# Expert visits of two half tiles of 64 rows, in two column tiles of TensorE with the weights moving

## The chip, the cores and the metric

One core of a Trainium2 chip runs the whole program in one launch. The metric is the device time in microseconds (us) of one execution; everything is in 32-bit floats.

## The reference, cut to what matters

A small vision model: patches are embedded (1184 tokens of 256 numbers: 32 images of 37), one layer of attention is added, then a mixture of experts:

```python
scores = sigmoid(x @ gate_weight.T)             # 32 experts in 4 groups; 6 of them chosen per token: topidx
g = einsum('th,ehi->tei', x, w_gate)            # hidden size 128
u = einsum('th,ehi->tei', x, w_up)
eo = einsum('tei,eih->teh', silu(g) * u, w_down)
routed = einsum('te,teh->th', cw, eo)           # cw: weight of the 6 chosen experts, else 0
shared = silu(x @ shared_w_gate) * (x @ shared_w_up) @ shared_w_down
lg = topidx[:, 0] // 2                          # one of 16 anchor experts, hidden size 64
anchor = ...                                    # the same form, with the weights of expert lg
out = routed + shared + 0.1 * anchor
```

So 7 x 1184 = 8288 (token, expert) pairs are computed: 7104 routed ones and 1184 anchor ones. How many pairs an expert gets is known only on the chip.

## The kernel before, in words

**Up to the experts** (about the first 200 us). Attention runs over 6 blocks of two tiles of 111 tokens. VectorE ranks the chosen experts block by block (`choose`, `place`), and GpSimd scatters each normed token row, with its weights and its destination rows, into `rows_d` in DRAM, where each of 48 lists (32 experts, 16 anchors) has a place for 1184 rows: 77 indirect DMAs (line 457). Before that SyncE has filled the first 256 rows of every list with zeros (line 378), and it loads all expert weights into `W` in SBUF: part early (line 380), the rest once the attention's buffers are dead (lines 392 and 398).

**The table** (lines 1441 to 1526, VectorE). From the counts of the 48 lists it works out, for each of 112 tiles of 128 rows, which weights it takes, where its rows start in `rows_d`, and which of its rows are valid. TensorE turns the columns into rows (`table_rows`, line 711), VectorE copies them to the SBUF table (line 1530, `table_ok`), and all engines read it into registers with `entry` (line 319, a TENSOR_LOAD on the queue of the engine). TensorE meanwhile finishes the shared expert and keeps itself busy (`stay_busy`) up to the first tile.

**The tiles.** 25 anchor tiles come first, then 87 routed ones: 24 full ones of one expert (F), and 32 packed ones (M) whose rows belong to several experts and which are summed from visits (M and 31 extra X). All the 128 rows of one tile meet the weights of one expert; in a visit of a packed tile the rows of the others are masked out by a weight of 0. For each tile i:

- SyncE loads 128 rows into one of 6 buffers `G` (`load_rows`, line 413), once TensorE has turned, and VectorE has read, the tile six before it; the first routed tile also waits for all scatters.
- TensorE turns the rows (`turn_rows`, 2 transposes, line 812), then computes gates and ups (`up`, line 823: the weights are stationary, the 128 turned rows move; 4 matmuls of 128 columns, 2 for an anchor), and one step later the down product (`down`, line 838: hidden values stationary, 256 columns of weights move).
- ScalarE copies the up weights of tile i+2 from `W` to `UPW` (`copy_up`, line 981), the turned rows from PSUM to `GT` (line 985), computes silu (line 990), and, for F tiles, weighs the result (line 995).
- VectorE multiplies silu and up (`hidden`, line 1597), takes the weights and destinations out of `G` (`take_columns`, lines 1566 and 1574), and adds the weighed result to the sums (`accumulate`, line 1589).
- GpSimd sends the sums, when complete, to `sums_d` in DRAM with an indirect DMA (line 483, 66 sends).

The order on TensorE is written out: `up(i)`, `turn_rows(i + 2)`, `down(i - 1)`. A 32-bit matmul stands in the trace as two records (a transpose as one).

**The end.** SyncE reads the seven results of each token back (`load_part`, line 419), one of them already 16 tiles before the end, VectorE adds them (line 1626), and the output is stored.

Of the kernel before, what the change touches and what calls it, by code (L numbers as in the profile page):

```python
# [17 lines left out]
F32 = mybir.dt.float32  # L18
I32 = mybir.dt.int32
# [42 lines left out]
DUMMY_ROW = P + LISTS * LIST_ROWS  # L62
# [7 lines left out]
ROWS_PACKED = -(-TOKENS * TOPK // P)  # L70
LAST_FILLED = TOKENS * TOPK % P
FULL = -(-(TOKENS * TOPK - EXPERTS * (P - 1)) // P)
MIXED = ROWS_PACKED - FULL
EXTRAS = EXPERTS - 1
ANCHOR_PACKED = -(-TOKENS // P)
ANCHOR_TILES = ANCHOR_PACKED + ANCHORS - 1
KINDS = "A" * ANCHOR_TILES + "FFX" * 12 + "XM" * 6 + "XMM" * 13
XT = len(KINDS)
INDEX = [KINDS[:i].count(k) for i, k in enumerate(KINDS)]
TILE_AXIS, EXTRA_AXIS = 1000, 2000  # L80
RING = D + 1
GB = 6
PL = 3 * EXPERTS + ANCHORS


def routed(i):
    return KINDS[i] != "A"


def summed(i):  # L90

    return KINDS[i] != "F"


def sums_before(i):
    return sum(summed(k) for k in range(i))


def copied_by_act(i):
    return KINDS[i] != "F"  # L100


def copies_before(i):
    return sum(copied_by_act(k) == copied_by_act(i) for k in range(i))


def number_of(i):

    return {"A": 0, "F": TILE_AXIS, "M": TILE_AXIS + FULL, "X": EXTRA_AXIS}[KINDS[i]] + INDEX[i]


FIRST_ROUTED = ANCHOR_TILES
EARLY_COLS = 19482
TRI4 = 3 * LISTS
SMALL = TRI4 + 23
PIECES = [[(0, 4), (4, 8), (8, NT)]] * (CHOICES - 1) + [[(0, 4), (4, 7), (7, 9), (9, 10), (10, NT)]]
assert KINDS.count("F") == FULL and KINDS.count("M") == MIXED and KINDS.count("X") == EXTRAS
assert all(KINDS[:i].count("X") >= min(EXTRAS, INDEX[i] + 1) for i in range(XT) if KINDS[i] == "M")
assert FULL * D <= ANCHOR_COLS and XT <= P
# [4 lines left out]
def build(nc, pt, wt, posr, brow, wqkv, wo, wg1, wg2, lnwb, gwt, gbias, sgu, sd, wx,  # L124
          ident_c, cmask_c, turn_c, parity_c, cs_c, before_c, small_c, out):
    with ExitStack() as ctx:
# [56 lines left out]
        def dense(*shape):  # L183
# [5 lines left out]
            if len(shape) == 2:  # L189
# [16 lines left out]
        mixed = spent[:, 0:MIXED * RING]  # L206
        mixed_rows = mixed.bitcast(I32)
# [5 lines left out]
        of_lists = small[:, 0:3 * LISTS].rearrange("p (q l) -> p q l", q=3)  # L213
        iota_a, base0, tri4 = small[:, LISTS:LISTS + ANCHORS], small[:, 2 * LISTS:3 * LISTS], small[:, TRI4:TRI4 + 16]
        pcol, number, of_number, tile_number, spare_row, last_tile, first_w = (small[:, TRI4 + 16 + q:TRI4 + 17 + q]
                                                                                  for q in range(7))
        ring = sb("ring", [P, ANCHOR_PACKED * RING])
        h = sb("h", [P, NT, D])
        ring_rows = ring[:, :].bitcast(I32)
        token_row = sb("token_row", [P, 2, NT], I32)  # L220
        to_rows = sb("to_rows", [P, NT])
        spare = sb("spare", [P, 2])
# [32 lines left out]
        whole = sb("whole", [P, 2 * LISTS], I32)  # L255
        tcol = sb("tcol", [P, 24])
        valid = turn
# [3 lines left out]
        def later(n):  # L261
# [6 lines left out]
        GT = later(2 * D).rearrange("p (u k s) -> p u k s", u=2, k=KC)  # L268
        S = later(2 * P).rearrange("p (u s) -> p u s", u=2)
        H = later(2 * P).rearrange("p (u s) -> p u s", u=2)  # L270
        tabs = e_sb[:, 0:at[0]]
        edges = later(2 * P).rearrange("p (u s) -> p u s", u=2)
        H_anchor = edges
        UPW = sb("UPW", [P, 2, UP_COLS])
        wcol = sb("wcol", [P, XT])
        tok_full = sb("tok_full", [P, FULL], I32)
        Y = W[:, 0:FULL * D].rearrange("p (f d) -> p f d", d=D)
        parts = W[0:TP, 0:CHOICES * NT * D].rearrange("p (c t d) -> p c t d", c=CHOICES, t=NT)

        B = [ctx.enter_context(nc.psum_tensor(f"B{i}", [P, 512], F32)) for i in range(8)]  # L280

        rows_d = nc.dram_tensor("rows_d", [DUMMY_ROW + 2 * P, ROW], F32).ap()
        sums_d = nc.dram_tensor("sums_d", [SPARE_ROW + P, D], F32).ap()
# [22 lines left out]
        g_ld = [sem(f"g_ld{u}") for u in range(GB)]  # L306
        edges_ok, valid_ok, mixed_zero = sem("edges_ok"), sem("valid_ok"), sem("mixed_zero")
        gt_by = {True: sem("gt_by_act"), False: sem("gt_by_dve")}
        T_ps, U_ps, silu_ok, H_ok, upw_ok, D_ps, Y_ok = (
            sem("T_ps"), sem("U_ps"), sem("silu_ok"), sem("H_ok"), sem("upw_ok"), sem("D_ps"), sem("Y_ok"))  # L310
        meta_ok, acc_ok, ring_ok, ids_ok, spared = sem("meta_ok"), sem("acc_ok"), sem("ring_ok"), sem("ids_ok"), sem("spared")
        sent_anchor, sent_full, sent_mixed = sem("sent_anchor"), sem("sent_full"), sem("sent_mixed")
# [4 lines left out]
        def entry(engine, q, i, top):  # L317

            return nc.values_load(table[0:1, q, bass.ds(i, 1)], engines=(engine,), min_val=0, max_val=top,  # L319
                                  skip_runtime_bounds_check_because="the table is computed within these bounds")  # L320
# [28 lines left out]
        def _(sp):  # L349
# [26 lines left out]
            of_list = rows_d[0:LISTS * LIST_ROWS, :].rearrange("(l r) n -> r l n", r=LIST_ROWS)  # L376
# [5 lines left out]
            for half in range(2):  # L382
                sp.dma_start(rows_d[DUMMY_ROW + half * P:DUMMY_ROW + (half + 1) * P, :], padrow[:, :]).then_inc(ini_d, 16)
# [17 lines left out]
            sp.wait_ge(ini_d, 16 * 4)  # L401
# [3 lines left out]
            def load_rows(i):  # L405
                if i == FIRST_ROUTED:
                    sp.wait_ge(scat, 16 * NT * TOPK)
                if i >= GB:

                    sp.wait_ge(T_ps, i - GB + 1)  # L410
                    sp.wait_ge(meta_ok, i - GB + 1)
                row = entry(mybir.EngineType.SP, 1, i, DUMMY_ROW + P)
                sp.dma_start(G[:, i % GB, :], rows_d[bass.ds(row, P), :]).then_inc(g_ld[i % GB], 16)
# [6 lines left out]

            for i in range(XT):
                load_rows(i)
                if i == XT - 16:
                    sp.wait_ge(sent_anchor, 16 * ANCHOR_PACKED)
                    sp.wait_ge(sent_full, 16 * FULL)
                    load_part(TOPK)
            sp.wait_ge(D_ps, XT)
            sp.wait_ge(sent_mixed, 16 * MIXED)
# [9 lines left out]
        def _(pool):  # L438
# [10 lines left out]
            pool.memset(ring[:, :], 0.0).then_inc(ring_ok, 1)  # L449
# [25 lines left out]
            pool.wait_ge(hs_ok, NB)  # L475
            pool.memset(spent[:, 0:until_scattered], 0.0).then_inc(mixed_zero, 1)
            pool.wait_ge(scat_anchor, 16 * NT)
            pool.wait_ge(scat, 16 * NT * TOPK)
            pool.wait_ge(ini_d, 16 * 4)
            pool.memset(spent[:, until_scattered:MIXED * RING], 0.0).then_inc(mixed_zero, 1)  # L480

            def send(rows, src, done):
                pool.indirect_dma_start(sums_d, bass.IndirectOffsetOnAxis(ap=rows, axis=0), src, None).then_inc(done, 16)  # L483

# [1231 lines left out]
```

## Time and profile before

| | us |
|---|---|
| median of 3 runs | 418.36 |
| lowest, highest | 414.25, 418.94 |
| span of the profiled execution | 412.1 |
| TensorE busy in it | 343.3 (83%) |
| VectorE busy | 278.0 (67%) |
| ScalarE busy | 190.0 (46%) |
| GpSimd busy | 181.7 (44%) |

The span runs from the first to the last instruction of one execution; its own time outside the span is not shown, and the median of the runs lies 6.3 us above the span. A matmul's length in the profile holds a fixed part in which the next one already streams: rates are read from start to start.

### The profile page before, as it was taken

How to read it: one execution, taken by the hardware profiler on the slowest of the kernel's cores; microseconds unless marked ns; L12 is line 12 of the kernel's file. 1: busy time of each engine (PE TensorE's matmuls, PEld its weight loads, DVE VectorE, ACT ScalarE, POOL GpSimd, SP SyncE). 2: the span in 40 equal slices, each digit the busy share in tenths (PEclk: the TensorE clock that was granted, in tenths of full speed). 3: DMA queues.
4: the chain of work that ended last, by engine and by line, in shares of the span. 5: the costliest groups of instructions: out<-in, count | busy, mean ns of one | idle time of the engine just before them, and what ended most of it. 6: DMA issues, size and time to landing. Idle time of an engine off the chain costs nothing.

```text
span 412.1 us, 8817 instructions
## 1 busy us (share of the span) xinstructions
PE 343.3 (83%) x2552; PEld 299.1 (73%) x2552; DVE 278.0 (67%) x1171; ACT 190.0 (46%) x471; POOL 181.7 (44%) x159
## 2 busy tenths in 40 slices
PE   5999999999899968773889999999999999994000
PEld 3786978779687857561677789999999999993000
DVE  0466789989798886798357775555565665666675
ACT  1152153441545233400157777777877777771000
POOL 6000000588888768767871374344422344433000
PEclk9999999999999997985989999999999999998555
DMA  7999999986698643694555576555555559531998
GB/s 234 298 335 335 329 341 328 420 320 119 123 337 252 126 96 86 218 387 137 152 162 130 167 214 180 162 158 165 165 145 162 166 155 291 168 113 58 303 303 245
DMA packets 55823, 88.44 MB, mean 215 GB/s; under 512 B 16145, under 2 KB 46521, under 8 KB 55513
## 3 DMA queue, kind: packets, MB, share of 16 engines
q1 hardware_dynamic: 38192, 67.66, 52.9%
q0 software_dynamic: 16720, 19.48, 17.8%
q10 hardware_dynamic: 864, 0.73, 0.6%
q8 instruction: 21, 0.34, 0.3%
q14 instruction: 26, 0.21, 0.2%
HBM read 50.62 MB, written 37.09 MB: 213 GB/s over the span
## 4 chain that ended last, share of the span: by engine, by line
PE 60%; DVE 20%; DMA 8%; issue 3%; ACT 3%; SPq 3%; DVEq 2%; POOLq 0%
PE B L823 20%; PE B L838 10%; PE B L514 6%; PE B L812 5%; DMA W<-sums_d 4%; PE B L549 4%; PE B L632 3%; PE B L598 2%; PE B L618 2%; DVEq L319 2%; DMA e_sb<-rows_d 2%; SPq L419 2%; DVE ring L1589 1%; PE B L656 1%; DMA W<-in_pt 1%
## 5 line engine op out<-in xcount | busy, mean ns | idle before, releaser
L457 POOL DMA_INDIRECT rows_d<-spent,slot x77 | 104.1, 1352 | 97.3 <-issue 90.9
L823 PEld LDWEIGHTS B<-e_sb,UPW 128*128 128x128 f32 x796 | 105.4, 193 | 10.7 <-issue 5.5
L823 PE MATMUL B<-e_sb,UPW 128*128 128x128 f32 x796 | 108.9, 278 | 1.5 <-issue 1.5
L1597 DVE TENSOR_TENSOR e_sb<-e_sb,B 128x128 f32<-128x128 f32 (+1 forms) x112 | 32.3, 288 | 62.2 <-ACT e_sb L990 55.8
L981 ACT COPY UPW<-W 128x512 f32 (+1 forms) x112 | 63.9, 570 | 22.2 <-issue 13.9
L838 PE MATMUL B<-W,e_sb 128*128 x224 | 69.3, 391 | 0.8 <-DVE e_sb L1597 0.8
L483 POOL DMA_INDIRECT sums_d<-spent x32 | 31.1, 972 | 48.7 <-DVE spent L1589 47.9
L812 PE MATMUL B<-ident,e_sb 128*128 128x128 f32 x224 | 43.1, 274 | 1.9 <-DMA e_sb<-rows_d 1.8
L990 ACT ACTIVATE e_sb<-B 128x128 f32<-128x128 f32 (+1 forms) x112 | 30.9, 276 | 22.2 <-PE B L823 20.8
L514 PE MATMUL B<-W 128*111 128x256 f32 (+1 forms) x132 | 34.2, 406 | 4.6 <-DMA W<-in_pt 4.5
L483 POOL DMA_INDIRECT sums_d<-W,tok_full x24 | 23.2, 966 | 30.3 <-ACT W L995 29.7
L838 PEld LDWEIGHTS B<-W,e_sb 128*128 128x128 f32 x224 | 34.0, 192 | 3.5 <-issue 1.7
L985 ACT COPY e_sb<-B 128x256 f32<-128x256 f32 x88 | 32.3, 367 | 4.6 <-PE B L812 4.6
L514 PEld LDWEIGHTS B<-W 128*111 128x111 f32 (+1 forms) x132 | 23.3, 184 | 12.2 <-DMA W<-in_pt 5.3
L1589 DVE SCALAR_TENSOR_TENSOR spent<-B,wcol,spent 128x256 f32<-128x256 f32 (+1 forms) x63 | 30.4, 482 | 1.7 <-DVE spent L1574 0.8
L812 PEld LDWEIGHTS B<-ident,e_sb 128*128 128x128 f32 x224 | 28.5, 144 | 2.3 <-DMA e_sb<-rows_d 2.1
L1626 DVE TENSOR_TENSOR h<-h,W 112x1024 f32<-112x1024 f32 (+3 forms) x23 | 23.2, 1047 | 8.4 <-DMA W<-sums_d 8.4
L1289 DVE TENSOR_TENSOR e_sb<-B,spent 111x444 f32<-111x444 f32 (+1 forms) x44 | 23.6, 597 | 4.1 <-PE B L598 4.1
L1566 DVE TENSOR_TENSOR wcol<-e_sb,turn 128x1 f32<-128x1 f32 x112 | 17.2, 153 | 4.0 <-PE B L812 3.8
L598 PE MATMUL B<-W 32*111 32x222 f32 (+1 forms) x176 | 15.5, 369 | 4.8 <-ACT W L909 4.8
L549 PE MATMUL B<-W 128*128 128x222 f32 (+1 forms) x96 | 18.1, 341 | 0.6 <-ACT W L886 0.6
L606 PE MATMUL B<-spent 128*128 128x256 f32 x70 | 18.6, 414 | 0.0
(250 smaller groups left out, 524.0 us busy)
## 6 DMA issues: line engine op xcount, KB each, us to landing
e_sb<-rows_d SPq DMA_DIRECT2D x112, 161.0 KB, 2.3
rows_d<-spent SPq DMA_DIRECT2D x2, 7728.0 KB, 44.4
W<-in_wx SPq DMA_DIRECT2D x1, 6643.0 KB
W<-sums_d SPq DMA_DIRECT2D x13, 448.0 KB, 9.4
W<-in_wx SPq DMA_DIRECT2D x10, 516.5 KB, 9.5
W<-in_wx SPq DMA_DIRECT2D x1, 4576.0 KB, 18.7
W<-in_pt SPq DMA_DIRECT2D x4, 666.0 KB, 6.9
W<-sums_d SPq DMA_DIRECT2D x7, 336.0 KB, 11.1
```

The costliest lines, as they stand in the source:

```text
L457: pool.indirect_dma_start(rows_d, bass.IndirectOffsetOnAxis(ap=slot[0:n, t, j:j + 1], axis=0), xrow[0:n, t, :], None).then_inc(done, 16)
L483: pool.indirect_dma_start(sums_d, bass.IndirectOffsetOnAxis(ap=rows, axis=0), src, None).then_inc(done, 16)
L514: m = pe.matmul(B[0][0:TILES[t], i * D:(i + 1) * D], patch_view(b)[:, c, at:at + TILES[t]], w_patch[:, c, :], start=c == 0, stop=c == PC - 1)
L549: m = pe.matmul(B[4 + half][:, c * BT:c * BT + n], w_qkv[:, k, lo:lo + P], xnT[:, k, 0:n], start=k == 0, stop=k == KC - 1)
L812: m = pe.transpose(B[i % 2][:, k * P:(k + 1) * P], G[:, i % GB, k * P:(k + 1) * P], ident[:, :])
L823: mm = pe.matmul(B[2 + i % 2][:, m * P:(m + 1) * P], UPW[:, i % 2, at:at + P], GT[:, i % 2, k, :], start=k == 0, stop=k == KC - 1)
L838: pe.matmul(B[6 + i % 2][:, 0:D], hid[:, i % 2, :], weights, start=True, stop=True).then_inc(D_ps, 1)
L981: act.copy(UPW[:, i % 2, 0:n], W[:, bass.ds(e, size)][:, 0:n]).then_inc(upw_ok, 1)
L985: act.copy(GT[:, i % 2, :, :].rearrange("p k s -> p (k s)"), B[i % 2][:, 0:D]).then_inc(gt_by[True], 1)
L990: act.activation(S[0:n, i % 2, :], B[2 + i % 2][0:n, 0:P], ACT.Silu).then_inc(silu_ok, 1)
L1589: dve.scalar_tensor_tensor(sums, B[6 + i % 2][:, 0:D], wcol[:, i:i + 1], sums, ALU.mult, ALU.add).then_inc(acc_ok, 1)
L1597: dve.tensor_tensor(out[0:n, i % 2, :], S[0:n, i % 2, :], ups, ALU.mult).then_inc(H_ok, 1)
```

## The change

Every visit now has two halves of 64 rows. Each half belongs to one list (expert or anchor), and each list is cut into halves, so nothing is packed or summed: 17 anchor visits and 71 routed ones, 88, each with two sets of weights. Visits go in 44 rounds of two (the ninth round, r = 8, holds the last anchor visit and the first routed one). In `up` and `down` the rows are stationary (64 columns each, one half in TensorE's columns 0 to 63, the other in 64 to 127), and the weights move. The first half's weights are read out of `W` through a register of TensorE; the second half's are copied before, the up part by VectorE (`stage_up`), the down part by ScalarE (`stage_down`). The hidden values now come out with the rows on partitions and are turned back (`turn_hidden`, `hidden_copy`) for the down product. The weight of each row is multiplied in with the hidden values. GpSimd sends the 88 results directly, with a spare destination for empty rows. The zero fill of a list is 64 rows in place of 256. In the last ScalarE and VectorE loops shown, one round runs in the order given. The table shrinks from some 80 VectorE instructions to 20 up to `cols_ok`. Row loads are four DMAs of 64 rows per round; there are still 6 buffers `G`, that is 3 rounds.

```diff
+ANCHOR_VISITS = -(-((TOKENS + ANCHORS * (HALF - 1)) // HALF) // 2)
+ROUTED_VISITS = -(-((TOKENS * TOPK + EXPERTS * (HALF - 1)) // HALF) // 2)
...
             sp.wait_ge(ini, 6)
-            for half in range(2):
-                sp.dma_start(of_list[half * P:(half + 1) * P, :, :],
-                             padrow[:, :].unsqueeze(1).to_broadcast([P, LISTS, ROW])).then_inc(empty, 16)
+            sp.dma_start(of_list[0:HALF, :, :], padrow[0:HALF, :].unsqueeze(1).to_broadcast([HALF, LISTS, ROW])).then_inc(empty, 16)
...
+            def load_rows(r):
+                if r == FIRST_ROUTED:
+                    sp.wait_ge(scat, 16 * NT * TOPK)
+                if r >= GB // 2:
+                    sp.wait_ge(T_ps, r - GB // 2 + 1)
+                    sp.wait_ge(meta_ok, r - GB // 2 + 1)
+                rows = [entries(mybir.EngineType.SP, 2 + half, r, LAST_ROW - HALF) for half in range(2)]
+                for j in range(2):
+                    for half in range(2):
+                        sp.dma_start(G[half * HALF:(half + 1) * HALF, (2 * r + j) % GB, :],
+                                     rows_d[bass.ds(rows[half][j], HALF), :]).then_inc(g_ld[r % (GB // 2)], 16)
...
+            for r in range(ROUNDS):
+                load_rows(r)
+                if r == ROUNDS - 4:
...
                     load_part(TOPK)
...
+            for v in range(VISITS):
+                if v % 2 == 0:
+                    pool.wait_ge(Y_ok, v // 2 + 1)
+                    pool.wait_ge(meta_ok, v // 2 + 1)
...
+                pool.indirect_dma_start(sums_d, bass.IndirectOffsetOnAxis(ap=row_to[:, v:v + 1], axis=0), results(v),
+                                        None).then_inc(done, 16)
...
-            stay_busy(12, 3, w_sgu)
+            stay_busy(7, 3, w_sgu)
             table_rows()
+            spread_columns()
             shared_down(3)
-            slot_bounds()
...
+            def up(r, own_weights):
+                pe.wait_ge(GT_ok, r + 1)
+                pe.wait_ge(up_staged, r + 1)
+                for j in range(2):
+                    hidden, size = widths(2 * r + j)
+                    first = W[:, bass.ds(own_weights[j], size)]
+                    second = up_w[:, (2 * r + j) % 4, :]
+                    n = 2 * hidden
+                    for k in range(KC):
+                        for half, w in enumerate((first, second)):
+                            lo = half * HALF
+                            m = pe.matmul(B[2 + r % 2][lo:lo + HALF, j * D:j * D + n], GT[:, r % 2, j, k, lo:lo + HALF],
+                                          w[:, k * n:(k + 1) * n], start=k == 0, stop=k == KC - 1, tile_position=(0, lo))
+                m.then_inc(U_ps, 1)
...
+            def turn_hidden(r):
+                pe.wait_ge(H_ok, r + 1)
...
+                for j in range(2):
+                    m = pe.transpose(B[4 + r % 2][:, j * P:(j + 1) * P], H[:, j, :], ident[:, :])
+                m.then_inc(HT_ps, 1)
+
+            def down(r, own_weights):
+                pe.wait_ge(HT_ok, r + 1)
+                pe.wait_ge(down_staged, r + 1)
...
+                    for half, w in enumerate((first, second)):
+                        lo = half * HALF
+                        m = pe.matmul(B[6 + r % 2][lo:lo + HALF, j * D:(j + 1) * D], HT[:, j, lo:lo + HALF], w,
+                                      start=True, stop=True, tile_position=(0, lo))
+                m.then_inc(D_ps, 1)
...
+            for r in range(ROUNDS):
+                own_weights = weights_of(mybir.EngineType.PE, 0, r)
+                up(r, own_weights)
+                if r >= 1:
+                    down(r - 1, before_own)
+                if r + 2 < ROUNDS:
+                    turn_rows(r + 2)
+                turn_hidden(r)
+                before_own = own_weights
+            down(ROUNDS - 1, before_own)
...
+            for r in range(ROUNDS):
+                hidden_silu(r)
+                if r >= 1:
+                    result_copy(r - 1)
+                hidden_copy(r)
+                if r + 2 < ROUNDS:
+                    turned_copy(r + 2)
+                if r + 1 < ROUNDS:
+                    stage_down(r + 1)
...
+            def stage_up(r):
+                places = weights_of(mybir.EngineType.DVE, 1, r)
...
+                if r >= 2:
+                    dve.wait_ge(U_ps, r - 1)
+                for j in range(2):
...
+                    m = dve.tensor_copy(up_w[:, (2 * r + j) % 4, 0:n], W[:, bass.ds(places[j], size)][:, 0:n])
+                m.then_inc(up_staged, 1)
+
+            def columns(r):
+                dve.wait_ge(T_ps, r + 1)
...
+                for j in range(2):
...
+                    m = dve.scalar_tensor_tensor(own[:, j, :, :], iota_to.unsqueeze(1).to_broadcast([P, 2, TO_ROW]),
+                                                 expert_col[:, v:v + 1], both, ALU.is_equal, ALU.mult)
+                step(m)
+                dve.reduce_sum(wcol[:, r % 2 * 2:r % 2 * 2 + 2], own[:, :, 0, :], axis=AX.X).then_inc(weight_ok, 1)
+                step(dve.reduce_sum(to_sum[:, :], own[:, :, 1, :], axis=AX.X))
+                dve.tensor_tensor(row_to[:, 2 * r:2 * r + 2], to_sum[:, :], spare_to[:, 2 * r:2 * r + 2], ALU.add).then_inc(meta_ok, 1)
+
+            def hidden(r):
...
+                for j in range(2):
...
+                    m = dve.scalar_tensor_tensor(H[:, j, 0:n], S[:, j, 0:n], wcol[:, v % 4:v % 4 + 1],
+                                                 B[2 + r % 2][:, j * D + n:j * D + 2 * n], ALU.mult, ALU.mult)
+                m.then_inc(H_ok, 1)
...
+            for r in range(ROUNDS):
+                hidden(r)
+                if r + 2 < ROUNDS:
+                    stage_up(r + 2)
+                if r + 1 < ROUNDS:
+                    columns(r + 1)
```

A row load, a register load (`entries`: one TENSOR_LOAD for two numbers), and a send keep their form; `turned_copy(r)` and `result_copy(r)` of ScalarE each copy 512 columns out of PSUM, `hidden_copy(r)` 256, `stage_down(r)` twice 256 out of SBUF, and `hidden_silu(r)` takes 256 columns.

## Rows read from the trace of the kernel before

**Rows 1.** Windows: length; PE, weight-load, DVE, ACT, POOL busy; clock share; DMA share; GB/s.

```profile
300.00:320.00 20.00, 20.00 (x158) 19.33 (x157) 12.47 (x53) 15.13 (x40) 5.79 (x6) 1.00 0.53 149
```

**Rows 2.** Timeline, TensorE, two routed tiles (start us, length us, engine, line, operation, count).

```profile
300.14 0.38 PE L812 MATMUL B<-ident,e_sb 128*128 128x128 f32 x2
...
300.36 0.60 PE L838 MATMUL B<-W,e_sb 128*128 x2
...
300.79 1.05 PE L823 MATMUL B<-e_sb,UPW 128*128 128x128 f32 x8
...
301.68 0.38 PE L812 MATMUL B<-ident,e_sb 128*128 128x128 f32 x2
```

**Rows 3.** Timeline, TensorE, end of the shared part and of the two kinds of tile.

```profile
192.59 1.87 PE L711 MATMUL B<-ident,tcol 128*1 128x128 f32 x8 [8.31 <-DVE tcol L1524]
...
203.14 0.41 PE L812 MATMUL B<-ident,e_sb 128*128 128x128 f32 x2
...
240.53 1.13 PE L823 MATMUL B<-e_sb,UPW 128*128 128x128 f32 x8
```

**Rows 4.** Timeline, VectorE and GpSimd, the table of tiles being built.

```profile
178.83 0.19 DVE L1441 SCALAR_TENSOR_TENSOR e_sb<-base,small 128x32 f32<-128x32 f32 x1
...
179.75 0.69 DVE L1447 CAST e_sb<-whole 128x32 f32<-128x32 int32 x1
...
179.11 1.35 POOL L457 DMA_INDIRECT rows_d<-spent,slot  x1 [2.69 <-DVE slot L1245]
...
214.50 3.26 POOL L480 MEMSET spent<- 128x3791 f32 x1 [2.10 <-issue]
```

**Rows 5.** Timeline, SyncE, reads of the results; TensorE, last product.

```profile
340.69 1.33 SPq L419 DMA_DIRECT2D W<-sums_d  x3
...
379.95 12.61 SPq L419 DMA_DIRECT2D W<-sums_d  x20
...
374.94 0.69 PE L838 MATMUL B<-W,e_sb 128*128 x2 [0.34 <-DVE e_sb L1597]
```

**Rows 6.** Groups by form: busy us, mean ns | idle before them.

```profile
L981 ACT COPY UPW<-W 128x512 f32 x87 | 53.8, 618 | 16.1 <-issue 9.8
...
L985 ACT COPY e_sb<-B 128x256 f32<-128x256 f32 x88 | 32.3, 367 | 4.6 <-PE B L812 4.6
...
L990 ACT ACTIVATE e_sb<-B 128x128 f32<-128x128 f32 x87 | 24.1, 278 | 15.8 <-PE B L823 14.9
...
L1597 DVE TENSOR_TENSOR e_sb<-e_sb,B 128x128 f32<-128x128 f32 x87 | 25.1, 288 | 54.1 <-ACT e_sb L990 54.1
...
L1589 DVE SCALAR_TENSOR_TENSOR spent<-B,wcol,spent 128x256 f32<-128x256 f32 x32 | 15.3, 479 | 0.5 <-PE B L838 0.5
```

**Rows 7.** Line 319 on SyncE, first tiles (duration ns min/median/max, first and last start).

```profile
L319 SPq TENSOR_LOAD <-scratch x7: 285/1075/1447, 195.3 to 205.3; - x7
```

**Rows 8.** Lines 319 and 413 over the span, same columns.

```profile
L319 SPq TENSOR_LOAD <-scratch x112: 262/268/1447, 195.3 to 363.0; - x112
...
L319 PEldq TENSOR_LOAD <-scratch x112: 296/302/1745, 206.1 to 373.6; - x112
...
L413 SPq DMA_DIRECT2D e_sb<-rows_d x112: 332/333/808, 196.8 to 363.4; - x112
...
DMA to landing us min/median/max: 2.2/2.3/6.2
```

**Rows 9.** Chain that ended last (start us, us, what), first rows from DRAM.

```profile
198.48 6.87 DMA e_sb<-rows_d
```

**Rows 10.** Timeline, TensorE, around the attention product in four column tiles.

```profile
110.11 1.50 PE L514 MATMUL B<-W 128*74 128x256 f32 x6
...
111.55 1.75 PE L618 MATMUL B<-e_sb,W 111*32 111x111 f32 x64
...
113.22 0.60 PE L539 MATMUL B<-ident,W 111*128 111x111 f32 x4
```

**Rows 11.** Page, group of the sends to DRAM.

```profile
L483 POOL DMA_INDIRECT sums_d<-spent x32 | 31.1, 972 | 48.7 <-DVE spent L1589 47.9
```

More of the change, by code:

```diff
@@ new lines, in stage_down @@
+            def stage_down(r):
+                places = weights_of(mybir.EngineType.Activation, 1, r)
+                if r == FIRST_ROUTED:
+                    act.wait_ge(ld["late0"], 16)
+                    act.wait_ge(ld["late1"], 16 * LATE_PIECES)
+                if r >= 2:
+                    act.wait_ge(D_ps, r - 1)
+                for j in range(2):
+                    hidden, size = widths(2 * r + j)
+                    n = KC * 2 * hidden
+                    m = act.copy(down_w[:, (2 * r + j) % 4, :], W[:, bass.ds(places[j], size)][:, n:n + D])
+                m.then_inc(down_staged, 1)
@@ L1422, in tab @@
                 return v
-            starts, ends, total, of_tile, mine = tab(PL), tab(PL), tab(E), tab(E), tab(PL)
-            facts = tab(4 * PL).rearrange("p (q l) -> p q l", q=4)
-            offset, many, shifted, slot_tile = (facts[:, q, :] for q in range(4))
-            held, begin, end, full, lead, behind = tab(LISTS), tab(LISTS), tab(LISTS), tab(E), tab(LISTS), tab(LISTS)
-            new, away, some, rounded, over, span, own = (tab(LISTS), tab(LISTS), tab(LISTS), tab(E), tab(E), tab(ANCHORS),
-                                                         tab(LISTS))
@@ L1447, in _ @@
-            step(dve.tensor_copy(full, whole[:, 0:E]))
-            dve.scalar_tensor_tensor(held[:, LR], full, -float(P), total, ALU.mult, ALU.add)
-            step(dve.tensor_tensor_scan(ends[:, R], ones_of, full, float(TILE_AXIS), ALU.mult, ALU.add))
-            dve.tensor_copy(first_c, ends[:, E - 1:E])
-            dve.tensor_scalar(some, held, 0.0, None, ALU.is_gt)
-            dve.tensor_tensor(starts[:, R], ends[:, R], full, ALU.subtract)
-            step(dve.tensor_tensor_scan(end[:, LR], ones_of, held[:, LR], 0.0, ALU.mult, ALU.add))
@@ new lines, in _ @@
+            for half in range(2):
+                m = dve.scalar_tensor_tensor(passed[:, half, :], ends, number[:, half:half + 1], ones[:, 0:LISTS], ALU.is_gt, ALU.mult)
+            step(m)
+            dve.scalar_tensor_tensor(facts[:, 0, :], starts, -float(HALF), base0, ALU.mult, ALU.add)
+            for half in range(2):
+                m = dve.scalar_tensor_tensor(mine[:, half, :], starts, number[:, half:half + 1], passed[:, half, :],
+                                             ALU.is_le, ALU.mult)
@@ new lines, in _ @@
+            step(m)
+            for half in range(2):
+                m = dve.tensor_tensor(picked[:, half, :, :], facts, mine[:, half, :].unsqueeze(1).to_broadcast([P, FACTS, LISTS]),
+                                      ALU.mult)
+            step(m)
+            step(dve.reduce_sum(picked_of[:, :, 0:FACTS], picked, axis=AX.X))
+            dve.tensor_scalar(weight_at[:, :], picked_of[:, :, 2], first_weight, None, ALU.add)
+            for half in range(2):
+                first, last = picked_of[:, half, 0:1], picked_of[:, half, 1:2]
+                m = dve.tensor_scalar(starting[:, half:half + 1], first, row_of_number[:, half:half + 1], last, ALU.add, ALU.min)
```

533 lines of the change are left out of this document (186 added, 347 removed).

## The prediction, made before the change was run

> **What bounds the kernel now.** I read the windows first, then the timeline of TensorE by stage, the chain that ended last, and the groups with their lengths.
>
> In the routed tiles TensorE is the bound: its busy share is 20.00 of 20 us, at the full granted clock, where VectorE has 12.47 and ScalarE 15.13 [rows 1]. One tile takes 301.68 - 300.14 = 1.54 us: two transposes 0.22 (0.11 each), the down product 0.43 (two records of 256 columns, 0.215 each), and 8 up records of 128 columns 0.89 (0.11 each) [rows 2]. So a record costs by its moving columns, and the 87 routed tiles cost 134 us. The 25 anchor tiles run from 203.14 to 240.53, 37.4 us, 1.5 each [rows 3]; there TensorE has only half the up records, and the chain goes through VectorE (register loads and sums) instead.
>
> Ahead of them TensorE waits 8.31 us for the table [rows 3], which VectorE builds from 178.83 [rows 4] until just before 192.59. After 374.94 + 0.69 = 375.6 only the results are read back, added and stored: 36.5 us to the end of the span at 412.1 [rows 5].
>
> **The table.** About 80 instructions in 13.7 us become 20. A small dependent instruction takes about 0.2 [rows 4]; by 8 dependent steps, a dozen others at 0.1, two products of 240 elements and a sum of 480 (0.3 to 0.6 each, between 288 ns for 128 elements and 479 for 256 [rows 6] and on at the same slope), I get 3.5, with one stall as of the cast at 179.75 (0.69 in place of 0.2) 4.0 us. So the columns are there at 182.8, not 192.5. TensorE then needed 203.14 - 192.59 = 10.55 us to the first turned rows; with the same shared parts left, that gives 193.4 for TensorE's side.
>
> What is late next are the rows. SyncE's first register loads take 1.08 us in the median, not 0.27 [rows 7, 8], and the first row loads 6.87 us to land, not 2.3 [rows 8, 9], while GpSimd's scatters run; those are not moved by the change, and their last data is in only by 214.5 [rows 4]. The table is in SBUF at about 185.5; two register loads and four issues of 0.33 plus 0.1 each make 3.8 us per round, so the first round's rows are issued by 189.5 and land at 196. By the same pace rounds 1 to 5 land at 200, 203.5, 207, 211 and 213.5. Round 3 thus cannot end before about 214.5. Four more anchor rounds at 2.7 (below) bring the first routed round to 225.3, against 240.5 before: 15 us gained. Lower bound if the loads come at the later pace: 221.
>
> **A routed round** (two visits), TensorE:
> - rows turned: 4 x 0.11 = 0.44, hidden turned: 2 x 0.11 = 0.22
> - up: 8 matmuls of 256 columns = 16 records; if the two halves stream side by side, 8 x 0.215 = 1.72
> - down: 8 records, side by side 4 x 0.215 = 0.86
> - two changes between the full array and the column tiles.
>
> Do they run side by side? The nearest rows are the attention product, in four column tiles of 32: 64 records in 1.75 us, that is (1.75 - 0.26) / 63 = 0.024 us from start to start [rows 10], where one record alone, by its 111 columns, is 0.11 x 111/128 = 0.095. That is four at a time. I take two at a time here. The other end is none: 3.44 and 1.72.
>
> The changes: into that product, the last record before it starts at 110.11 + 1.50 - 0.38 = 111.23, streams 0.215, and the product starts at 111.55, 0.1 late; out of it, the last record starts at 113.04, streams 0.095, and the next is at 113.22, 0.09 late [rows 10]. 0.1 each, bounds 0 and 0.2. Sum: 0.44 + 0.22 + 1.72 + 0.86 + 0.2 = 3.44 us. An anchor round has up at half, 2.6.
>
> **Three other loops come out as long.**
> (a) Hidden values. From the last up record: 0.17 until it is readable, silu of 256 columns 0.38 (278 ns for 128, 367 for a copy of 256 [rows 6]), two products of 128 on VectorE 0.56 (0.21 from start to start and 0.35, from 288 and 479 ns [rows 6]), hand-overs 0.1: 1.21. TensorE has the down product and the turning of rows meanwhile, 1.4, so this alone is covered. But `weights_of` stands behind `turn_hidden`, which waits for H: the queue's register load of 0.30 [rows 8] and its address arithmetic come after that wait, about 0.46, and only then can `up` go: 1.21 + 0.46 + 1.72 + 0.1 for the change = 3.49.
> (b) Rows. Behind VectorE's `columns` (about 1.5 to 1.9 us after the hidden values are turned, since the staging copies stand ahead of them) SyncE needs two register loads (0.27), and four issues (0.33 and 0.1 each), 2.1, and the data 2.3 [rows 8]. The rows must be there 0.83 before the end of the round two later: (1.5..1.9 + 4.4 + 0.83) / 2 = 3.4 to 3.6. Before, each tile had one issue and six tiles of slack.
> (c) ScalarE: 0.28 + 0.49 + 0.27 + 0.49 + 2 x 0.31 = 2.2 of start-to-start time (each length of its kind less 0.1 [rows 6]) and GpSimd 2 x (0.97 + 0.3) = 2.5 [rows 11] stay below. In anchor rounds ScalarE's order (hidden copy, turned copy, staging, then silu) sets about 2.7.
> VectorE: hidden 0.56, a register load 0.35, two copies of 512, columns 0.95. The copy isn't in the trace at that size; it lies between 0.2 (the small instructions [rows 4]) and 0.96 (twice the 479 ns of 256 elements [rows 6]); I take 0.45 each, between them, so 2.8, which is below; with the upper end it would be 3.8.
>
> With three loops at 3.4 to 3.6 and none with slack I take 3.6, bounds 3.44 and 4.1 (the rows' landing one us later). 36 rounds (r = 8 to 43): 129.6 us, ending at 354.9.
>
> One more stall: `load_part` of the last choice stands in SyncE's queue ahead of the row loads of the last three rounds. It issues for 1.33 us [rows 5] and moves 1.2 MB beside them. Six tiles of slack hid it; here I put 3 us, bounds 0 and 5.
>
> **The end.** After the last `turn_hidden`: copy 0.4, down 0.86, 0.17: 1.5. Then a result copy and two sends (0.97 + 0.3 + 0.97) in place of a sum, a fix-up and one send: +0.4 on the 36.5. The reading back is unchanged.
>
> **Sum.** 225.3 + 129.6 + 1.5 + 3 + 36.9 = 396.3, against 412.1: 15.8 us less. The median stands 6.3 above the span and I carry that over: 418.36 - 15.8 = 402.6, so 402 us.
>
> **Edits at nothing.** The smaller zero fill: GpSimd's scatters start sooner, but before the last 18 of them GpSimd had already caught up and waited 2.69 us for the last slots [rows 4], so those are released at the same time either way. Masks for empty rows go into the hidden product. ScalarE's staging lies under TensorE's 3.44; if that cover went it would cost 0.6 a round.
>
> **A rule weighed.** The cast at 179.75 ended at 180.44, with GpSimd's indirect DMA that ran from 179.11 to 180.46 [rows 4]: a copy within SBUF waits for GpSimd. `stage_up` is such a copy, and two sends per round run beside it. The Trainium skill, page "SBUF — State Buffer", section on the port pair that VectorE and GpSimd share, has it as an exclusive lock for the whole instruction, whichever comes first. By that rule both copies could wait out a send, which is rival 3; the trace agrees with the direction, 0.5 us lost once.
>
> **Rivals.**
> 1. *Everything at its lower bound.* First routed round at 221, 3.44 a round, no stall of `load_part`: 221 + 123.8 + 1.5 + 36.9 = 383.2, time 389. For it: TensorE held 1.54 a tile without a gap [rows 1, 2]. Against: loop (a). Chance 0.17.
> 2. *The row loads take over.* Landing one us later, or columns that late, makes 4.1 a round: +18, time 420. For it: four issues in place of two, and half the slack. Against: the loads land in 2.3 us in the median at a DMA share of 0.53 [rows 1, 8]. Chance 0.12. The Trainium skill, page "SBUF — State Buffer", section on issuing two DMAs to hit both halves, says that a transfer of 64 partitions reaches half of the DMA ports and that two such transfers do not run side by side; by it a half load would take about as long as a full one, so the four loads of a round would fill the engines as four tiles did. The trace has no load of 64 rows; the sum takes the full load's 2.3 us for each.
> 3. *VectorE is locked out by GpSimd.* Each copy waits out a whole send of 0.97 [rows 11]: 2.8 + 1.9 = 4.7 a round, +1.1 x 36 = 40: 442. It makes VectorE the bound from 0.8 us of waiting a round on, and eats the gain from 1.3. Against: the cast waited 0.5, not a whole transfer. Chance 0.05.
> 4. *The column tiles take turns* (slower). Up 3.44, down 1.72: 6.0 a round, +2.4 x 36 = 87, anchors +1.7 x 8 = 14: about 503. It decides from the point where the records start 0.13 apart on average, not 0.11 (24 of them a round, 0.44 us). Against: the attention product [rows 10]. Chance 0.04.
>
> Forecast 402, chance 0.62, own range 394 to 411.
>
> **Chances.** A measurement tells about 2% here: faster is below 410, slower above 426.7. Faster: 0.9 of the forecast and rival 1, 0.73. Within 2%: the rest of the forecast and rival 2, 0.17. Slower: rivals 3 and 4 and a part for causes not seen, 0.10. Range 388 to 419: rival 1 and most of rival 2.
>
> **What would show it.** Up records of the two halves starting about 0.11 apart; rounds of 3.6; the table's first transfer at 183; the first routed `up` near 225; row loads with little waiting of SyncE for `columns`. Wrong would be: gaps before `up` with TensorE waiting for rows (rival 2), staging copies of over 1 us (rival 3), starts 0.215 apart (rival 4).

## The result, and the profile after

The changed kernel took 446.51 us in the median (444.15 to 449.19, 4 runs) beside 418.65 for the kernel before (414.25 to 420.54, 4 runs): a ratio of 1.070, 95% interval 1.062 to 1.078. It is slower by 7%, where 402 us had been predicted. Its profiled execution spans 447.4 us, before 412.1. The first is the slowest of its four runs (449.19) and the second the fastest of its four (414.25), so the spans lie 35 us apart and the medians 28. Marks of that execution beside those of the prediction:

| mark | predicted, us | measured, us |
|---|---|---|
| table in SBUF | 185.5 | 189.0 |
| first round's row loads issued | 189.5 | 197.3 |
| first rows there | 196 | 202.7 |
| first routed `up` | 225.3 | 247.2 |
| from there to the end of the last `down` | 134.1 | 158.7 |
| from there to the end | 36.9 | 41.5 |
| span | 396.3 | 447.4 |

TensorE's time, in windows of the routed rounds (the columns are those of [rows 1]):

```profile
300.00:320.00 20.00, 15.86 (x132) 10.25 (x132) 11.15 (x45) 10.69 (x27) 10.12 (x10) 1.00 0.48 142
320.00:340.00 20.00, 17.23 (x148) 11.06 (x145) 9.70 (x38) 11.61 (x30) 8.37 (x9) 1.00 0.46 134
340.00:360.00 20.00, 17.13 (x145) 11.09 (x145) 10.84 (x43) 11.70 (x30) 10.12 (x10) 1.00 0.47 136
```

TensorE has lost the full busy share of [rows 1] at the same granted clock, and no engine has taken its place: the highest of the others is at 11.7 of 20. So a wait bounds these rounds. The timeline of TensorE's `up` shows that it isn't the column tiles (`W` feeds the first half's, `up_w` the second's):

```profile
303.06 0.38 PE L806 MATMUL B<-W,e_sb 128*64 x1
303.07 0.38 PE L806 MATMUL B<-up_w,e_sb 128*64 128x256 f32 x1
303.27 0.38 PE L806 MATMUL B<-W,e_sb 128*64 x1
303.29 0.38 PE L806 MATMUL B<-up_w,e_sb 128*64 128x256 f32 x1
```

The two halves start 0.01 us apart and the pairs 0.21: two weight matrices stream at once, at the pace of one in [rows 2]. What TensorE waits for stands in the waits (us in total, times, longest; the weight loads, PEld, and the matmuls wait for the same rows):

```profile
PEld B L790 <- DMA e_sb<-rows_d: 45.2, 23, 7.2
PE B L790 <- DMA e_sb<-rows_d: 41.3, 21, 6.8
```

SyncE's two lines (the source views of lines 406 and 303; duration ns min/median/max) are to be held against [rows 8]:

```profile
L406 SPq DMA_DIRECT2D e_sb<-rows_d x176: 468/468/1479, 194.1 to 391.8; - x176
...
L303 SPq TENSOR_LOAD <-scratch x88: 463/489/2515, 191.4 to 389.0; - x88
```

A load of 64 rows holds SyncE longer than one of 128 did (0.468 against 0.333 us), and a register load of two values costs 0.489 where one value cost 0.268. What stands ahead of the prediction says that a row load and a register load keep their form; their shape is another, and so is SyncE's time for them. The chain that ended last shows the whole step, from the `columns` of round 19 to those of round 22 (L1513 is their last instruction):

```profile
294.42 0.17 DVE turn L1513
...
295.89 0.47 SPq L406
...
296.54 0.47 SPq L406
...
297.19 0.47 SPq L406
...
297.85 3.88 DMA e_sb<-rows_d
...
301.77 0.66 PE B L790 x4
...
307.25 0.17 DVE turn L1513
```

The issues start 0.65 apart. A round is 4 x 0.65 + 2 x 0.49 = 3.6 us of SyncE's queue, and the last of the four loads lands 3.88 after its issue (3.46 to 4.07 at the four such places of the chain between 250 and 300 us). From `columns` to `columns` it is 307.42 - 294.59 = 12.83 us for three rounds, since there are three rounds of buffers: 4.28 a round. The turned rows of rounds 10 and 43 start at 250.59 and 395.80, so a routed round takes 145.21 / 33 = 4.40 us; up to round 39 (375.03), ahead of the reading of the last choice, it is 4.29.

SyncE itself is nearly full. Its own waits between 250 and 380 us are 11.4 us in 130 (us in total, times, longest; line 402 is its wait for `columns`):

```profile
SPq L402 <- DVE turn L1513: 11.0, 15, 1.8
SPq L303 <- PE B L790: 0.4, 1, 0.4
```

The start, from the same chain and TensorE's timeline:

```profile
183.01 8.41 DMA rows_d<-spent,slot
...
191.44 1.22 SPq L303
...
192.69 1.21 SPq L303
...
197.34 1.91 SPq L303
...
199.28 2.27 SPq L303
```

```profile
202.71 1.09 PE L790 MATMUL B<-ident,e_sb 128*128 128x128 f32 x4 [6.48 <-DMA e_sb<-rows_d]
210.59 1.11 PE L790 MATMUL B<-ident,e_sb 128*128 128x128 f32 x4 [6.79 <-DMA e_sb<-rows_d]
217.56 1.12 PE L790 MATMUL B<-ident,e_sb 128*128 128x128 f32 x4 [3.32 <-DMA e_sb<-rows_d]
```

The table is ready at 189.0, but SyncE stands at `scat_anchor` until the last scatter of anchor rows has landed, 8.41 us after its start. Then each register load takes 1.2 to 2.5 us while GpSimd scatters, and the first three rounds come 7 to 8 us apart.

### The profile page after: what moved, and what is told of

Its sections match the earlier page's. It is cut to its first block, busy times and chain, and to the rows that moved or that the text cites. A ratio compares the mean times of both kernels' runs of the same rounds, so it can differ in the third digit from the quotient of the medians.

```text
span 447.4 us, 8558 instructions
## 1 busy us (share of the span) xinstructions
PE 334.5 (75%) x2622; PEld 246.5 (55%) x2622; DVE 263.1 (59%) x1053; ACT 170.2 (38%) x400; POOL 199.4 (45%) x178
## 4 chain that ended last, share of the span: by engine, by line
PE 28%; DVE 16%; issue 16%; DMA 14%; POOL 10%; SPq 10%; ACT 3%; DVEq 1%; POOLq 0%; ACTq 0%
POOL sums_d L474 10%; PE B L490 6%; DMA e_sb<-rows_d 6%; DMA W<-sums_d 5%; SPq L406 4%; SPq L303 4%; PE B L806 3%; PE B L525 3%; PE B L594 2%; DMA rows_d<-spent,slot 2%; PE B L608 2%; PE B L574 2%; SPq L413 1%; PE B L790 1%; PE B L632 1%
## 5 line engine op out<-in xcount | busy, mean ns | idle before, releaser
L474 POOL DMA_INDIRECT sums_d<-spent,turn x56 | 57.5, 1027 | 71.2 <-ACT spent L1002 51.3
L806 PE MATMUL B<-W,e_sb 128*64 x352 | 81.7, 378 | 6.8 <-issue 4.2
L806 PE MATMUL B<-up_w,e_sb 128*64 128x256 f32 (+1 forms) x352 | 81.9, 379 | 0.0
L806 PEld LDWEIGHTS B<-W,e_sb 128*64 128x64 f32 x352 | 45.6, 143 | 30.9 <-issue 16.7
L474 POOL DMA_INDIRECT sums_d<-W,turn x32 | 32.6, 1018 | 36.4 <-ACT W L1002 31.5
L832 PE MATMUL B<-W,HT 128*64 x176 | 47.6, 395 | 0.5 <-ACT HT L995 0.5
L832 PE MATMUL B<-down_w,HT 128*64 128x256 f32 x176 | 47.6, 395 | 0.0
L806 PEld LDWEIGHTS B<-up_w,e_sb 128*64 128x64 f32 x352 | 45.6, 143 | 0.0
L1497 DVE COPY up_w<-W 128x512 f32 (+1 forms) x88 | 31.9, 404 | 10.6 <-issue 9.6
L1015 ACT COPY down_w<-W 128x256 f32 x88 | 31.7, 414 | 1.9 <-issue 1.7
```

Source lines behind the costliest of these rows:

```text
L806: m = pe.matmul(B[2 + r % 2][lo:lo + HALF, j * D:j * D + n], GT[:, r % 2, j, k, lo:lo + HALF], w[:, k * n:(k + 1) * n], start=k == 0, stop ...
L832: m = pe.matmul(B[6 + r % 2][lo:lo + HALF, j * D:(j + 1) * D], HT[:, j, lo:lo + HALF], w, start=True, stop=True, tile_position=(0, lo))
L1015: m = act.copy(down_w[:, (2 * r + j) % 4, :], W[:, bass.ds(places[j], size)][:, n:n + D])
L1497: m = dve.tensor_copy(up_w[:, (2 * r + j) % 4, 0:n], W[:, bass.ds(places[j], size)][:, 0:n])
```

## The experiments

**Theory A**: SyncE's own time for half-row loads (two addresses, four issues a round) delays the rows. **Theory B**: the rows' landing and the three rounds of buffers do. **Theory C**: GpSimd's sends do. All times are medians; ratios are to the kernel before, with 95% intervals. Four versions (one_addr, one_load, full, full_deep_ahead) leave out the rows of each visit's second list: its partitions are filled by the first half's address, and results go to fixed rows. They don't give the reference's values, and tell of time alone.

**one_addr.** One address for both halves:

```diff
-rows = [entries(mybir.EngineType.SP, 2 + half, r, LAST_ROW - HALF) for half in range(2)]
+rows = entries(mybir.EngineType.SP, 2, r, LAST_ROW - HALF)
...
-                 rows_d[bass.ds(rows[half][j], HALF), :])
+                 rows_d[bass.ds(rows[j], HALF), :])
```

> Both halves of a visit read the 64 rows of the first half's address, so SyncE needs one register load a round in place of two; the four 64-row loads stay, and sends go to fixed rows of their own (values of the result are not computed). Theory A (rows are late because SyncE itself is busy about 3.6 us a round: 2 register loads of about 0.48 and 4 issues of about 0.65): 0.5 us less on SyncE in each of the 44 rounds, 20 us less at most, 427 to 434. Theory B (the rows' landing of 3.5 to 3.9 us and three rounds of buffers set the loop, SyncE's own time little): half of that, 435 to 441. Theory C (GpSimd's sends set the loop): 446.

432.84 us, ratio 1.036 (1.026 to 1.045): 13.7 less than the changed kernel, as A has it; C expected nothing. But B is not out by it: at the three routed places of this chain (245 to 280 us) the last load lands 2.42 to 2.74 us after its issue, in place of 3.46 to 4.07, so the edit shortened the landing too. Why is not shown.

**deep.** `GB = 8` for 6, that is four rounds of buffers, with small tiles moved to make room.

> The whole computation; four rounds of row buffers in place of three, the rest unchanged. Theory A: SyncE's 3.6 to 3.7 us a round remain as a floor, so rounds fall from 4.5 to 3.8 at best: 420 to 430, and SyncE has no idle time. Theory B: one more round of slack hides the landing altogether: 410 to 420. Theory C: 446.

435.41, ratio 1.042 (1.034 to 1.050): 11.1 less, a miss for A's range and for B's. TensorE's timeline says why:

```profile
299.16 0.66 PE L790 MATMUL B<-ident,e_sb 128*128 128x128 f32 x4
...
303.03 0.66 PE L790 MATMUL B<-ident,e_sb 128*128 128x128 f32 x4
...
306.89 0.66 PE L790 MATMUL B<-ident,e_sb 128*128 128x128 f32 x4
```

From 256 us to the reading of the last choice the rounds are 3.87 us without a wait for rows, though SyncE's work is the same: its 3.6 just keeps up (it waits for 1.0 us in all from 256 to 380). So in the routed rounds it was SyncE's time, the landing and the three rounds of buffers together that made 4.3. But the anchor rounds, where TensorE needs less, and the start stay SyncE's: the first rows are turned at 203.43, and those of round 10 at 247.71. Depth helps only where SyncE's time is below TensorE's.

**two_queues.** Of each round's four loads, the second half's two and their register load go to ScalarE's queue, behind `stage_down(r + 1)`:

```diff
+                if r + GB // 2 < ROUNDS:
+                    load_second(r + GB // 2)
```

> The whole computation; the second half's rows are loaded by ScalarE's queue (its own register load and two issues, behind the staging copy of each round), the first half's by SyncE. Theory A: SyncE falls to 1.8 us a round; ScalarE rises from about 2.4 us of work to 4.2 with 0.5 for the load and 1.3 for the issues, so rounds of 3.9 to 4.3: 425 to 437. Theory B: the same rows land no sooner: 440 to 447. Theory C: 446 or above.

506.77, ratio 1.214 (1.203 to 1.225): a miss for A and B. It is above 446, as C says, but not through the sends, which are not in the loop that its chain shows. That chain goes round once in 310.11 - 304.19 = 5.9 us (ACTq is ScalarE's queue, with its register load at line 303 and its issues at line 989):

```profile
304.19 0.66 PE B L788 x4
304.85 0.23 PE B L814 x2
...
305.10 0.37 ACT HT L1008
...
305.93 0.64 ACTq L303
...
306.74 0.48 ACTq L989
...
307.38 2.68 DMA e_sb<-rows_d
...
310.11 0.84 PE B L788 x4
```

The load of round r+3 stands behind ScalarE's copy of round r's hidden values, which TensorE turns only behind the rows of round r+2. So one whole landing lies in each round. It says where not to put a load; it doesn't speak against A. With half the loads in each queue, a load of 64 rows lands in 2.3 to 2.4 us in the median, as one of 128 did in [rows 8].

**one_load.** One load per visit that reads its 64 rows twice, to fill 128 partitions:

```diff
+sp.dma_start(G[:, (2 * r + j) % GB, :],
+             rows_d[bass.ds(rows[j], HALF), :].unsqueeze(0).to_broadcast([2, HALF, ROW]))
```

> As the variant with one address, and each visit's 128 partitions are filled by one load that reads its 64 rows twice: one register load and two issues a round in place of two and four. Theory A: SyncE's time falls to 1.8 us a round, rounds come to about 3.6 us from 4.5, and the start gains some us: 405 to 415. Theory B: as A if a load of 128 partitions lands in 2.3 us as before, else 435. Theory C: 446, since the sends are as many.

594.85, ratio 1.424 (1.412 to 1.436), a miss for all three. It tells nothing of A or B, since this form of load is itself slow. The issue takes 2.28 us in the median, and the chain has:

```profile
359.59 14.60 DMA e_sb<-rows_d
```

**full.** The same question with a source of 128 consecutive rows:

```diff
-        for half in range(2):
-            sp.dma_start(G[half * HALF:(half + 1) * HALF, (2 * r + j) % GB, :],
-                         rows_d[bass.ds(rows[half][j], HALF), :])
+        sp.dma_start(G[:, (2 * r + j) % GB, :], rows_d[bass.ds(rows[j], P), :])
```

> The changed kernel with one load of 128 consecutive rows for each visit (one address) in place of two of 64: the upper half of the partitions gets the wrong rows, and results are sent to fixed rows of their own, so the values are not the reference's; the filling of the lists with zeros covers 128 rows in place of 64, and all else is as in the changed kernel. Theory A (SyncE's own time for half-row loads is the bound): SyncE needs 0.49 + 2 x 0.5 = 1.5 us a round in place of 3.6; routed rounds fall from 4.4 to 3.87 on average, the anchor rounds and the start gain 10 us: 412 to 422, near the kernel before. Rival (the landing of rows and the sends set it): 440 to 446.

420.49, ratio 1.011 (1.004 to 1.019): 26.0 less, as A has it. The row bytes and the sends are as many, and the zero fill is twice as large, so neither is the cause. What has shrunk is SyncE's work and, with it, the landing, 2.4 us in the median; how much of the 26 each is worth was not separated. Its source view:

```profile
L405 SPq DMA_DIRECT2D e_sb<-rows_d x88: 332/333/1542, 191.3 to 360.9; - x88
...
DMA to landing us min/median/max: 2.2/2.4/6.0
```

From round 12 to the reading of the last choice the rounds are 3.87 us without a wait for rows. Half of the gain lies ahead of them: the rows of round 10 are turned at 236.61 (250.59 in the changed kernel).

**before_halves.** The converse, in the kernel before: each tile's 128 rows by two loads of 64, nothing else.

```diff
-sp.dma_start(G[:, i % GB, :], rows_d[bass.ds(row, P), :])
+for half in range(2):
+    sp.dma_start(G[half * P // 2:(half + 1) * P // 2, i % GB, :],
+                 rows_d[half * P // 2:, :][bass.ds(row, P // 2), :])
```

> The kernel before, with each tile's 128 rows loaded by two loads of 64 rows instead of one of 128; nothing else is touched. Theory A (a load of 64 rows costs SyncE its own 0.65 us, as much as one of 128 or more): SyncE needs 0.27 + 2 x 0.65 = 1.6 us a tile against TensorE's 1.54, so the routed tiles grow by 0 to 6 us and the start, where SyncE is slow, by some us more: 420 to 432. Theory B (half loads cost half): 418 to 420.

453.68, ratio 1.082 (1.074 to 1.089): a miss for A and B, and this one edit costs more than the whole change. The price of a load was right, its effect not. The chain is SyncE's from one tile to the next, 305.90 - 304.22 = 1.68 us:

```profile
304.22 0.28 SPq L319
...
304.67 0.47 SPq L414
...
305.32 0.47 SPq L414
...
305.90 0.26 SPq L319
```

Against TensorE's 1.54 that is 0.14 a tile, 12 us in 87 tiles; I had judged by 0.06. But the queue is the bound from the first tile: from 196 to 405 us it waits for a free buffer only seven times, 2.2 us in all.

```profile
SPq L319 <- PE B L814: 2.2, 7, 0.6
```

Its loads run from 200.1 to 404.6, 1.83 a tile over 112 tiles, 38 us longer than before (196.8 to 363.4). Whatever makes one of its steps longer (issues take up to 1.62 us) is never won back. Before, SyncE's work for a tile took 0.78 us, and it caught up within some ten tiles. Here nothing but SyncE's own time is left as the bound.

**deep_four and deep_ahead**, each on top of deep. The first fetches a round's four addresses with one register load; the second moves TensorE's:

```diff
-own_weights = weights_of(mybir.EngineType.PE, 0, r)
+own_weights = ahead
...
+if r + 1 < ROUNDS:
+    ahead = weights_of(mybir.EngineType.PE, 0, r + 1)
 turn_hidden(r)
```

> The variant with four rounds of row buffers, where SyncE fetches a round's four addresses with one register load in place of two. With that depth the rounds run at 3.87 us without waiting for rows, so none are gained there if TensorE's own loop sets them (theory A); the start gains one slow register load (1.5 to 2.3 us) in each of the first three rounds, and the three rounds behind the reading back of the last choice a little: 427 to 432, against 435.4. If SyncE's time still set the rounds (rival), another 0.4 in each: 415 to 420.

> The variant with four rounds of row buffers, where TensorE's register load of the next round's places stands ahead of the turning of the hidden values in place of behind it. If the 3.87 us of a round are TensorE's own sum (1.95 + 0.86 + 0.59 + 0.23) and 0.25 of waiting behind that load (theory A), a round takes 3.6 to 3.65: 0.22 to 0.25 in each of some 38 rounds, 8 to 10 us less than 435.4: 425 to 428. If the hidden values' chain through ScalarE and VectorE sets the 3.87, the time stays at 435.

deep_four: 431.97, ratio 1.035 (1.026 to 1.044), within what A expects, but not for the reason given, and its 3.4 us less than deep lie within the spread of its own runs (431.06 to 437.24): the one load isn't cheap. The source view of the version itself reads

```profile
L403 SPq TENSOR_LOAD <-scratch x44: 886/984/3281, 191.6 to 370.3; - x44
```

(in best2, which has it too, the median is 0.902). So it is 0.268 and 0.489 us for one and two values, and 0.90 to 0.98 for four: 0.21 to 0.24 for each further value. The Trainium skill, page "Runtime: NRT & Kernel Launch", section "Instruction fetch mechanics", gives about 200 ns a register, in bulk too, for register loads from HBM; these rows, from a table in SBUF, agree.

deep_ahead: 430.71, ratio 1.029 (1.023 to 1.036), 4.7 less where 8 to 10 were expected. Undisturbed rounds fall from 3.87 to 3.54 as forecast (295.44, 298.99, 302.53), but then SyncE's 3.6 is above them, so every third or fourth waits for rows again. The mean is (358.54 - 244.89) / 30 = 3.79 up to round 40, and 3.94 with the reading of the last choice.

**full_deep_ahead.** Whole loads, four rounds of buffers and the load ahead together.

> The same loads of 128 rows with four rounds of row buffers and TensorE's register load ahead of the turning of the hidden values: the round that the change would have had with whole loads. Theory A: 3.55 us a round from the start on, no wait for rows: 36 x 0.32 = 11 us less than the variant with whole loads alone, 400 to 410, which is what had been forecast for the change. Rival: as deep_ahead, 430.

402.39, ratio 0.970 (0.962 to 0.978), as A has it. TensorE is the bound again, at 20.00 of 20 us and 3.545 us a round from round 10 to the last, without a stall at the last choice. The sends are the same 88, so they don't set the changed kernel's rounds, and C falls.

```profile
280.00:300.00 20.00, 20.00 (x172) 12.81 (x169) 12.40 (x51) 13.56 (x35) 10.92 (x12) 1.00 0.52 163
300.00:320.00 20.00, 20.00 (x172) 12.87 (x172) 12.91 (x52) 13.88 (x35) 11.23 (x12) 1.00 0.56 174
```

**late_part.** The changed kernel with `if r == ROUNDS - 1:` for `ROUNDS - 4` ahead of `load_part(TOPK)`.

> The changed kernel with the last choice's results read back after the last row loads in place of ahead of the last three rounds'. If that stall costs what the trace shows (the rounds at 375 to 392 us take 4.5 us more than the mean) and the reading finds its place beside the last rounds: 441 to 443. If the stall is taken over by SyncE's queue at the end: 446.

442.34, ratio 1.063 (1.051 to 1.076): 4.2 less, as expected, but the interval is about 5 us to either side, so it is not clear of the noise.

**best1 and best2**, the whole computation. best1: deep_four with the load ahead, and the second half's loads of rounds 0 to 2 on ScalarE's queue, which has nothing else to do there. best2: rounds 0 to 3, and `load_part` late.

> The whole computation: four rounds of row buffers, one register load a round on SyncE, TensorE's register load ahead, and in the first three rounds the second half's rows loaded by ScalarE's queue, which is idle there. By theory A the three gains add: 435.4 less 9 for the load ahead, less 5 for SyncE's register loads, less 5 to 7 at the start for ScalarE's help: 412 to 420, that is within 2% of the kernel before, not clearly faster. If they don't add, 420 to 428.

> best1 with ScalarE's help in the first four rounds in place of three, and the last choice's results read back after the last row loads. Expected by theory A: 5 us less for the stall and 1 to 3 at the start, 412 to 416. If the start is set by the scatters' own traffic, whoever issues the loads: 415 to 417.

best1: 420.54, ratio 1.002 (0.998 to 1.006), just above what A expects. best2: 413.71, ratio 0.991 (0.986 to 0.996), as A has it: 1% below the kernel before, less than the 2% that count here as faster, and 33 us faster than the changed one. TensorE has 19.33 us in its window from 300 to 320, and rows are still waited for in 20.7 us.

## Why the prediction was wrong

**The step that failed** is loop (b) of the routed round and its twin at the start: "SyncE needs two register loads (0.27), and four issues (0.33 and 0.1 each), 2.1, and the data 2.3". I took the rows of loads of other shapes: 0.268 is for one value, 0.333 for 128 partitions. They measured 0.489, and 0.65 from start to start: 3.6 us of SyncE's queue a round, and 3.5 to 4.1 for the last landing, not 2.3. The loop was right in kind, and its first term too: `columns` ends 1.7 us behind the turning of the hidden values (292.87 to 294.59), for 1.5 to 1.9. But from there to the turned rows it was 301.77 - 294.59 = 7.2, where I had 4.4. With that, three rounds of buffers no longer cover it, and at the start and in the anchor rounds SyncE's queue alone is the bound. Whole loads took away 26 us (full), one address for both halves 13.7 (one_addr), a fourth round of buffers 11.1 (deep). That SyncE's own time can be the bound by itself is shown in before_halves; in the changed kernel its share and the landing's were not separated.

- **The start** (+21.9 us). The table's cost was right: the columns took from 182.74 to 187.08, 4.3 us for 4.0. Of its gain 2.4 us were lost at a gate that I had left out, the landing of the last anchor scatter at 191.4. The first rows were turned 6.7 us later than forecast, and the other 15 were lost up to the first routed `up`: "3.8 us per round at the start" was 7 to 8, since each register load took up to 2.5 us, where I had 1.08, the median for one value. The anchor rounds, put at 2.7 by ScalarE, then ran at SyncE's pace.
- **TensorE's sum of 3.44** was 0.1 short: 3.545 in full_deep_ahead. The column tiles side by side (rival 4 falls) and the half-size up of anchors were right.
- **Loop (a), 3.49**, was right in kind, with `weights_of` behind `turn_hidden` as its last link, and short in size: 3.87 in deep and full. TensorE's register load of two values takes 0.53, where I had 0.30. Moving it brought 3.54.
- **Rival 2** (the row loads take over, chance 0.12) was the case that came. Its 4.1 a round was too low (4.40), and it had nothing at the start.
- **Rival 3** didn't come, but these runs hardly test it. The staging copy took 0.42 us in the median and 0.57 at most:

```profile
L1497 DVE COPY up_w<-W x88: 274/422/572, 192.8 to 396.6; 128x512 f32 x71, 128x256 f32 x17
```

No pair of copies started while a send ran: the send comes behind ScalarE's result copy, when VectorE is copying already. There the send is the longer one:

```profile
313.65 0.76 DVE L1497 COPY up_w<-W 128x512 f32 x2 [0.33 <-issue]
314.03 1.23 POOL L474 DMA_INDIRECT sums_d<-W,turn  x1 [1.47 <-ACT W L1002]
```

A send beside no copy takes 0.97. So what a copy does that meets a running send is not shown here; the order of the two kept the case from coming up.

- **The rule weighed under rival 2** was worth more than I gave it. With two half loads a round in each queue (two_queues) half a load takes as long to land as a whole one, 2.3 to 2.4 us, and the last of four in one queue took 3.5 to 4.1, which agrees with it. The Trainium skill says it outright on page "DMA: Bandwidth & Descriptors", section "Rules for kernel authors": don't split a transfer by partition halves, use one of 128. What I had priced by the wrong row was the issuing engine's time.
- **`load_part`**: 3 us foreseen, 4.2 measured, with an interval of about 5 to either side.
- **The end** (+4.6): GpSimd's four sends behind the last product end 4.4 us after it, at 410.4; the reading back then took 35.5 us in place of 32.2, which I didn't trace.
- **The last slots** were written by VectorE at 182.54, not 178.63. That is no effect of the change: before_halves, which is the kernel before up to there, had them at 182.32, and the twelve profiled executions of the changed kernel and its versions between 180.05 and 183.03. The one execution of before from which the prediction started was an early one. Between 80 and 100 us and between 120 and 140 the granted clock was 1.00 in it, and 0.91 and 0.93 in the changed kernel's, 0.91 and 0.92 in that of before_halves; deep and one_addr, with 1.00 there, had the slots at 180.81 and 181.01. What makes up the other 2 us is open.

So what the change asks of TensorE holds, and what it asks of SyncE doesn't. That full_deep_ahead comes to the 402 us of the forecast is partly chance: it has a fourth round of buffers, an earlier register load and loads that can't carry two lists, its first routed `up` is at 229.86, 4.6 later than forecast, and from there to the last `down` it needs 128.7, 5.4 less.

## What to carry to other kernels

When a change turns one load into two of half the size, price the issuing queue, not the bytes: the issue and the address values it fetches, in the new shape, against what the compute engine takes for the same work. A queue above that is the bound from the first tile on, and lost time in it is not won back; deeper buffers help only where it is below. Check every gate ahead of a step that gets faster (here the scatter's landing) before counting its gain.

## What was not expected of the hardware

- The issue of a load of 64 partitions took 0.468 us, one of 128 partitions with the same row length 0.333, both in the same version of the kernel but for that edit (before_halves and before; the changed kernel and full).
- A register load on SyncE costs by its values: 0.268 us for one, 0.489 for two (0.70 in the median where it is the round's only one, in full and one_addr), 0.90 to 0.98 for four. It took 1.2 to 4.4 us instead of 0.5 to 0.9 while GpSimd issued indirect scatters.
- A load of 161 KB from a source of two blocks of 64 rows (the same rows twice) landed 14.6 us after its issue in the chain of one_load, where two such loads are issued together; one from a block of 128 lands in 2.4 in the median (full).
- A send of GpSimd that starts while VectorE copies 512 columns within SBUF took up to 1.23 us in place of 0.97.
